# The experts' first layer turned around: its hidden units on partitions, each tile's weights first copied to a fixed place

## The chip, the cores and the metric

The kernel runs on one core of a Trainium2 chip. The metric is the device time of one execution in microseconds (us). The core has five engines that run their own instruction streams and meet at semaphores: TensorE (PE in the profile, its weight loads PEld), VectorE (DVE), ScalarE (ACT), GpSimd (POOL) and SyncE (SP, which here issues most of the transfers).

## The reference

Two decoder layers on 4 sequences of 512 tokens of width 128, in float32. Each layer has self-attention, cross-attention to 77 context vectors, and a feed-forward part, each behind a layer norm and added to the residual. The feed-forward part of the first layer is a mixture of 8 experts, of which each token uses its two best:

```python
weights, indices = jax.lax.top_k(gate_logits, 2)
weights = jax.nn.softmax(weights, axis=-1)
h = einsum('bsd,edh->ebsh', x, w1) + b1      # 128 -> 1024 per expert
xh, gh = split(h, 2)                         # plain half, gated half: 512 each
act = silu(gh) * xh
out_e = einsum('ebsf,efd->ebsd', act, w2) + b2   # 512 -> 128
# the outputs of a token's two experts, weighed and summed
```

## The kernel before

The kernel is one program without loops at run time. Its first stream is the first layer's self-attention (A0) and cross-attention (X0), cut into 32 units of four heads. Then comes the expert stage (M0), then a second stream with self-attention (A1), cross-attention and feed-forward of the second layer.

**First stream.** For each unit SP loads the stacked queries and keys into one of four slots of the tile `stk` (`load_sp`, lines 638 and 644), and TensorE can't begin the unit's row maxima (L574) until both have landed. Between these loads SP issues, two per unit and in the order of a list called `later`, the weights that later stages need (`unit_sp`, L1173), and one piece of the experts' weights per unit (L2257). All these transfers go through one SP queue. One entry of `later` is the bias `b_gated`, the gated half of the experts' first bias, broadcast to all 128 partitions: 2 MB.

**Expert stage.** The 4096 pairs of token and expert are sorted by expert on the chip. GpSimd writes each token's normalised row to a region of its expert in device memory (`scatter_pool`, L1726: 32 indirect DMAs). Then 39 tiles of 128 rows follow, each of one expert. Which expert is known only at run time, so the engines read ten codes into registers (`codes`, L1686), each code holding the experts of four tiles, and address weights and biases through registers. A tile t goes through these steps:

1. SP loads its rows into `x_in` (L1833), TensorE transposes them (`turn`, L1753), and DVE copies the result to SBUF and computes where the outputs go (`turned`, L1637 and L1638).
2. TensorE multiplies them with the expert's first weights (`hidden`, L1759), the gated half (z=1) and the plain half (z=0). The rows stand on the partitions of the result, the 512 units on its free axis. Each half is one matmul of 128x512 in the program, which the profile shows as two instructions (float32).
3. DVE adds the gated bias (`gated`, L1644), ACT applies Silu (`gate_part`, L1802).
4. DVE adds the plain bias (L1651) and multiplies by the gate (L1655), both in `product`.
5. TensorE transposes the four 128x128 blocks of the activations (`turn_act`, L1767), ACT copies them to SBUF (`turned_act`, L1806), and TensorE multiplies them with the second weights (`output`, L1774: four accumulating matmuls, eight instructions).
6. DVE adds the second bias (L1661), and GpSimd scatters the tile's rows to device memory (L1742, an indirect DMA).

The order on each engine is written out by hand. TensorE: gated half of t+1, transposes of t's activations, `turn` of t+2, plain half of t+1, output of t. DVE: gated bias of t+1, `turned` of t+2, product of t+1, output bias of t. GpSimd does nothing in the stage but the scatter of each tile. An engine issues its instructions strictly in this order, so a wait holds everything behind it.

Of the kernel before, what the change touches and what calls it, by code (L numbers as in the profile page):

```python
# [11 lines left out]
F32 = mybir.dt.float32  # L12
# [239 lines left out]
def build(nc, d, out):  # L252
# [4 lines left out]
    with es:  # L257
# [71 lines left out]
        b1_gated = sb("b1_gated", [P, NE, FF])  # L329
        b1_plain = stk[:].rearrange("p u z h n -> p (u z h n)").bitcast(F32).rearrange("p (e n) -> p e n", e=NE)  # L330
# [1152 lines left out]
        def second_stream_sp(e):  # L1483
# [13 lines left out]
            diff expo plus recip gates zeroed scattered xT xT_out gated_half gated plain_half plain silu act actT actT_out y_in y_out  # L1497
# [86 lines left out]
        def moe_dve(e, ln):  # L1584
# [50 lines left out]
            def turned(t):  # L1635
                e.wait_ge(m["xT"], t + 1)
                e.tensor_copy(x_inT[:, t % 2], bank_misc[:, 0:P]).then_inc(m["xT_out"], 1)  # L1637
# [3 lines left out]
            def gated(t, ex):  # L1641
                k = t % 2
                e.wait_ge(m["gated_half"], t + 1)
                e.tensor_tensor(silu[:, k], hid[k][1], b1_gated[:, bass.ds(ex[t], 1)].rearrange("p o n -> p (o n)"), ALU.add)\  # L1644
                    .then_inc(m["gated"], 1)
# [18 lines left out]
            e.wait_ge(s_biases, 16 * 2)  # L1664
# [5 lines left out]
            gated(0, ex)  # L1670
            product(0, ex)
            for t in range(BUSY_TILES):
                if t + 1 < BUSY_TILES:
                    if t + 1 not in ex:
                        ex |= experts(code, t + 1)
                    gated(t + 1, ex)
# [29 lines left out]
        act = oT[:, 0]  # L1706
        actT = okT
# [5 lines left out]
        hid = [(bank_max[0], bank_max[1]), (bank_st[1], bank_st[2])]  # L1713
        y_bank = bank_st[0]
        t_bank = bank_st[3]
# [21 lines left out]
        def moe_pool(e, ln):  # L1737

            for t in range(BUSY_TILES):
                e.wait_ge(m["y_at"], t + 1)  # L1740
                e.wait_ge(m["y_out"], FREE + t + 1)
                e.indirect_dma_start(scr_y, bass.IndirectOffsetOnAxis(ap=y_at[:, t:t + 1], axis=0),  # L1742
                                     y_sb[:, t % 2], None).then_inc(m["stored"][t % 2], 16)

        def moe_pe(e, ln):
            weights_pe(e)
            e.wait_ge(m["tile_e"], CODED + 2)
            code = codes(e)

            def turn(t):  # L1750
                e.wait_ge(m["tile_in"][t % 2], 16 * (t // 2 + 1))
                wait(e, m["xT_out"], t)
                e.transpose(bank_misc[:, 0:P], x_in[:, t % 2, 0:D], ident[:]).then_inc(m["xT"], 1)  # L1753

            def hidden(t, ex, z):
# [3 lines left out]
                e.matmul(hid[t % 2][z], x_inT[:, t % 2],  # L1759
                         w1[:, bass.ds(ex[t], 1), z * FF:(z + 1) * FF].rearrange("p o n -> p (o n)"),  # L1760
                         start=True, stop=True).then_inc(m["gated_half" if z else "plain_half"], 1)

            def turn_act(t):
                e.wait_ge(m["act"], t + 1)
                wait(e, m["actT_out"], t)
                for c in range(FC):
                    mm = e.transpose(t_bank[:, c * P:(c + 1) * P], act[:, c * P:(c + 1) * P], ident[:])  # L1767
                mm.then_inc(m["actT"], 1)

            def output(t, ex):  # L1770
                e.wait_ge(m["actT_out"], t + 1)
                e.wait_ge(m["y_out"], FREE + t)
                for c in range(FC):
                    mm = e.matmul(y_bank[:, 0:D], actT[:, c * P:(c + 1) * P],  # L1774
                                  w2[:, bass.ds(ex[t], 1), c, :].rearrange("p o n -> p (o n)"), start=(c == 0), stop=(c == FC - 1))
# [5 lines left out]
            ex = experts(code, 0)  # L1781
            for z in (1, 0):
                hidden(0, ex, z)
            for t in range(BUSY_TILES):
                if t + 1 < BUSY_TILES:
                    if t + 1 not in ex:
                        ex |= experts(code, t + 1)
                    hidden(t + 1, ex, 1)
                turn_act(t)
                if t + 2 < BUSY_TILES:  # L1790
                    turn(t + 2)
                if t + 1 < BUSY_TILES:
                    hidden(t + 1, ex, 0)
                output(t, ex)

        def moe_act(e, ln):
            e.wait_ge(m["diff"], 1)
            e.activation(gate_t[:, 1], gate_t[:, 0], ACT.Exp).then_inc(m["expo"], 1)

            def gate_part(t):  # L1800
                e.wait_ge(m["gated"], t + 1)
                e.activation(silu[:, t % 2], silu[:, t % 2], ACT.Silu).then_inc(m["silu"], 1)  # L1802

            def turned_act(t):
                e.wait_ge(m["actT"], t + 1)
                e.copy(actT[:], t_bank).then_inc(m["actT_out"], 1)  # L1806

            gate_part(0)
            for t in range(BUSY_TILES):
                turned_act(t)  # L1810
                if t + 1 < BUSY_TILES:
                    gate_part(t + 1)
# [150 lines left out]
        def weights_pe(e):  # L1963
            e.wait_ge(f["abs"], 2)
# [274 lines left out]
        halves = d["M0_b1"].rearrange("o (e z n) -> o e z n", e=NE, z=2)  # L2239
        later += [(b1_gated[:], halves[:, :, 1].to_broadcast([P, NE, FF]))]  # L2240
# [148 lines left out]
```

## Time and profile before

| | |
|---|---|
| median of 3 runs | 846.29 us (845.27 to 852.08) |
| profiled execution, span from first to last instruction | 844.2 us |
| first half-matmul of the expert stage to end of its last scatter | 371.8 to 504.7 us |

| busy, us (share of the span) | |
|---|---|
| PE | 689.9 (82%) |
| DVE | 589.3 (70%) |
| ACT | 414.1 (49%) |
| POOL | 285.0 (34%) |

The profile shows one execution and gives no other time for it than its span, so what lies around the span is taken as the 2.1 us between it and the median. The shares are means over stages that have different limits; what the change does is read in the stretches where it acts. The TensorE clock that the chip granted has two levels, 1.2 GHz (0.50) and 2.4 GHz (1.00); over the whole span its mean is 0.88.

### The profile page before, as it was taken

How to read it: one execution, taken by the hardware profiler on the slowest of the kernel's cores; microseconds unless marked ns; L12 is line 12 of the kernel's file. 1: busy time of each engine (PE TensorE's matmuls, PEld its weight loads, DVE VectorE, ACT ScalarE, POOL GpSimd, SP SyncE). 2: the span in 40 equal slices, each digit the busy share in tenths (PEclk: the TensorE clock that was granted, in tenths of full speed). 3: DMA queues.
4: the chain of work that ended last, by engine and by line, in shares of the span. 5: the costliest groups of instructions: out<-in, count | busy, mean ns of one | idle time of the engine just before them, and what ended most of it. 6: DMA issues, size and time to landing. Idle time of an engine off the chain costs nothing.

```text
span 844.2 us, 14947 instructions
## 1 busy us (share of the span) xinstructions
PE 689.9 (82%) x4693; PEld 333.1 (39%) x4698; DVE 589.3 (70%) x1606; ACT 414.1 (49%) x708; POOL 285.0 (34%) x504
## 2 busy tenths in 40 slices
PE   2759999989888998239999973668899988999887
PEld 1334454444434445116666641212232322324443
DVE  3757678686646664738788753778889898962664
ACT  1332556555665443003333322137688787885454
POOL 4742454543532233723222320122423133230310
PEclk9875999998988657569999995559999999999998
DMA  7443665482232314311111113521122210000000
GB/s 217 150 176 107 190 183 155 125 262 78 83 93 53 94 47 128 96 36 38 43 41 45 39 29 105 169 75 52 63 90 89 64 52 26 26 2 1 0 26 26
DMA packets 74780, 71.27 MB, mean 84 GB/s; under 512 B 14560, under 2 KB 67168, under 8 KB 74704
## 3 DMA queue, kind: packets, MB, share of 16 engines
q1 hardware_dynamic: 72000, 64.84, 25.1%
q0 software_dynamic: 2272, 4.69, 1.8%
q8 instruction: 40, 0.66, 0.3%
q10 hardware_dynamic: 432, 0.79, 0.3%
q14 instruction: 36, 0.29, 0.1%
HBM read 41.90 MB, written 28.00 MB: 83 GB/s over the span
## 4 chain that ended last, share of the span: by engine, by line
PE 62%; DVE 18%; issue 7%; POOL 4%; DMA 4%; ACT 4%; SPq 1%; DVEq 0%; POOLq 0%; ACTq 0%
PE bank_pv L732 11%; DVE mx L590 9%; PE bank_turn L574 8%; PE bank_scores L2024 5%; PE bank_scores L684 4%; PE bank_scores L1774 4%; PE bank_turn L1759 4%; PE bank_scores L1759 4%; PE bank_turn L751 3%; POOL routed_tokens L1726 2%; PE bank_scores L1767 2%; PE bank_turn L793 2%; PE bank_turn L528 2%; DMA stk<-stack_A 1%; DVE stats L450 1%
## 5 line engine op out<-in xcount | busy, mean ns | idle before, releaser
L590 DVE TENSOR_REDUCE mx<-bank_turn 128x1 f32<-128x512 f32 (+3 forms) x452 | 260.6, 616 | 67.2 <-PE bank_turn L579 35.8
L574 PE MATMUL bank_turn<-stk 64*128 64x77 bf16 (+4 forms) x708 | 164.2, 314 | 29.4 <-DVE mx L590 17.7
L684 PE MATMUL bank_scores<-stk 64*128 64x512 bf16 (+4 forms) x576 | 176.4, 372 | 4.8 <-ACT probs L705 3.6
L709 ACT ACTIVATE probs<-bank_scores 128x1024 f32<-128x1024 f32 (+4 forms) x160 | 117.2, 768 | 111.7 <-PE bank_scores L684 111.4
L705 ACT ACTIVATE probs<-bank_scores 128x512 f32<-128x512 f32 x256 | 138.6, 605 | 35.3 <-PE bank_scores L684 34.3
L732 PE MATMUL bank_pv<-probs,vsl 128*32 128x512 f32 (+4 forms) x1152 | 143.0, 570 | 2.8 <-POOL probs L717 1.9
L574 PEld LDWEIGHTS bank_turn<-stk 64*128 64x128 bf16 x708 | 54.4, 102 | 134.5 <-DVE mx L590 63.2
L717 POOL TENSOR_SCALAR_AFFINE_SELECT probs<-probs 128x256 f32<-128x256 f32 x128 | 52.1, 410 | 78.1 <-ACT probs L709 76.8
L1742 POOL DMA_INDIRECT expert_outputs<-probs,y_at x39 | 37.4, 960 | 101.0 <-DVE probs L1661 98.0
L477 POOL TENSOR_TENSOR rstd<-var,mhalf 128x4 f32<-128x4 f32 x24 | 25.4, 1058 | 119.2 <-DVE var L456 119.1
L1806 ACT COPY okT<-bank_scores 128x512 f32<-128x512 f32 x39 | 22.9, 587 | 80.8 <-PE bank_scores L1767 80.8
L528 PE MATMUL bank_turn<-ident,xn 128*128 128x128 f32 x60 | 13.2, 358 | 57.0 <-DVE xn L471 57.0
L684 PEld LDWEIGHTS bank_scores<-stk 64*128 64x128 bf16 (+1 forms) x576 | 47.6, 97 | 30.0 <-ACT probs L705 18.0
L579 PE MATMUL bank_turn<-behind_even,even_q 64*128 64x128 bf16 x256 | 53.4, 230 | 0.0
L578 PE MATMUL bank_turn<-behind_pair,pair_q 64*128 64x128 bf16 x256 | 53.4, 230 | 0.0
L1774 PEld LDWEIGHTS bank_scores<-w,okT 128*128 128x128 f32 x312 | 37.7, 191 | 25.0 <-issue 25.0
L2024 PE MATMUL bank_scores<-f_w1c,w 128*128 128x512 f32 x96 | 46.0, 616 | 0.4 <-ACT w L537 0.4
L1774 PE MATMUL bank_scores<-w,okT 128*128 x312 | 43.9, 284 | 0.8 <-ACT okT L1806 0.8
L604 POOL CAST neg<-mx 128x16 bf16<-128x16 f32 x33 | 6.5, 198 | 111.5 <-DVE mx L590 98.1
L590 DVE TENSOR_REDUCE mx<-bank_scores 128x1 f32<-128x512 f32 x60 | 40.8, 680 | 3.0 <-PE bank_scores L574 2.9
L1759 PE MATMUL bank_turn<-w,probs 128*128 x80 | 42.5, 616 | 0.0
L542 ACT COPY xnT<-bank_turn 128x512 f32<-128x512 f32 x19 | 11.1, 584 | 56.9 <-PE bank_turn L528 56.9
(299 smaller groups left out, 1179.7 us busy)
## 6 DMA issues: line engine op xcount, KB each, us to landing
stk<-stack_A SPq DMA_DIRECT2D x64, 256.0 KB, 3.2
w<-in_M_w SPq DMA_DIRECT2D x12, 512.0 KB, 4.7
stack_A<-parts SPq DMA_DIRECT2D x15, 384.0 KB, 3.1
stack_A<-fill SPq DMA_DIRECT2D x8, 512.0 KB, 5.1
stk<-stack_X SPq DMA_DIRECT2D x16, 256.0 KB, 2.7
stack_A<-parts SPq DMA_DIRECT2D x15, 256.0 KB, 3.2
probs<-routed_tokens SPq DMA_DIRECT2D x39, 65.0 KB, 1.8
b_gated<-in_M_b SPq DMA_DIRECT2D x1, 2048.0 KB, 11.9
```

The costliest lines, as they stand in the source:

```text
L574: mm = e.matmul(o, stk[r, slot, 0, pp, qt * P:(qt + 1) * P], stk[r, slot, 1, pp, 0:keys], start=True, stop=not a.causal)
L578: e.matmul(o, half(pair_q, j), half(behind_pair, j), start=False, stop=False)
L579: mm = e.matmul(o, half(even_q, j), half(behind_even, j), start=False, stop=True)
L590: e.tensor_reduce(o.rearrange("p h q -> p q h"), bank_of((g, m))[:, 0:k * keys].rearrange("p (q h k) -> p q h k", q=len(tiles), h=len(hs)) ...
L684: mm = e.matmul(score_bank(g, kt, i)[0:a.kp, 0:S - q0], stk[r, slot, 1, pp, kt * P:kt * P + a.kp], stk[r, slot, 0, pp, q0:S], start=True, ...
L705: e.activation(probs[:, probs_of(g, kt), j + 2 * pp], score_bank(g, kt, i), ACT.Exp, scale=1 / math.sqrt(HD)).then_inc(s["probs"], 1)
L709: e.activation(probs[0:a.kp, probs_of(g, kt), j:HG:2, 0:n], bank_scores[0:a.kp, 2 * j:2 * j + 2, 0:n], ACT.Exp, scale=1 / math.sqrt(HD)).t ...
L717: e.affine_select(out=o, in_=o, compare_op=ALU.is_ge, fill=0.0, base=0, pattern=[[0, 2], [1, P]], channel_multiplier=-1).then_inc(s["maske ...
L732: mm = e.matmul(bank_pv[VW * h:VW * (h + 1), q0:S], vsl[0:a.kp, slot, kt, h, :], probs[0:a.kp, probs_of(g, kt), h, 0:S - q0], start=(kt == ...
L1759: e.matmul(hid[t % 2][z], x_inT[:, t % 2], w1[:, bass.ds(ex[t], 1), z * FF:(z + 1) * FF].rearrange("p o n -> p (o n)"), start=True, stop=T ...
L1774: mm = e.matmul(y_bank[:, 0:D], actT[:, c * P:(c + 1) * P], w2[:, bass.ds(ex[t], 1), c, :].rearrange("p o n -> p (o n)"), start=(c == 0), ...
L2024: e.matmul(bank, f_xT[:, b, j * P + tap:j * P + tap + P], f_w1c[:, tap], start=(tap == 0), stop=False)
```

## The change

Layout: the first layer's weights become the stationary operand and the tokens the moving one, so the 512 units of a half come out on partitions, in four blocks of 128, and the tokens on the free axis. This is the layout that the second layer needs: `turn_act` and `turned_act` (L1767, L1806) go. A bias is now one value per partition: ACT adds the gated bias inside Silu, DVE adds the plain bias inside the product, each in four instructions, one per block of 128 units. The bias is loaded as 64 rows of 128 and transposed once by TensorE; the two broadcast loads of 2 MB (`b_gated` in `later`, and `b1_plain` at the start of `moe_sp`, L1816) go.

Weights: GpSimd copies the 128x1024 first weights of a tile's expert into one of two fixed places (`w_now`), so TensorE's first layer needs no registers. GpSimd now reads the codes itself. Its order is: copy of t+2, scatter of t, copy of t+3, scatter of t+1, and so on; ACT reads the codes too.

Order: DVE keeps `turned` of t+2, product of t+1, output of t. TensorE keeps gated half of t+1, `turn` of t+2, plain half of t+1, output of t. `act` is double, the gated half has one bank, the plain half two.

```diff
+        w_now = sb("w_now", [P, 2, 2 * FF])
+        b1_rows = sb("b1_rows", [NE * 2 * FC, P])
+        b1_cols = sb("b1_cols", [P, NE, 2 * FC])
...
             def product(t, ex):
                 e.wait_ge(m["plain_half"], t + 1)
-                wait(e, m["act"], t)
-                e.tensor_tensor(act[:], hid[k][0], b1_plain[:, bass.ds(ex[t], 1)].rearrange("p o n -> p (o n)"), ALU.add)\
-                    .then_inc(m["plain"], 1)
-                e.wait_ge(m["plain"], t + 1)
                 e.wait_ge(m["silu"], t + 1)
-                e.tensor_tensor(act[:], act[:], silu[:, k], ALU.mult).then_inc(m["act"], 1)
+                wait(e, m["y_in"], t - 1)
+                for c in range(FC):
+                    cols = slice(c * P, (c + 1) * P)
+                    i = e.scalar_tensor_tensor(act[:, k, cols], plain_bank[k][:, cols],
+                                               b1_cols[:, bass.ds(ex[t], 1), c], silu[:, k, cols], ALU.add, ALU.mult)
+                i.then_inc(m["act"], 1)
...
-            gated(0, ex)
             product(0, ex)
...
         def moe_pool(e, ln):
+            def weights(t, ex):
+                wait(e, m["plain_half"], t - 1)
+                e.tensor_copy(w_now[:, t % 2], w1[:, bass.ds(ex[t], 1)].rearrange("p o n -> p (o n)")).then_inc(m["w_now"], 1)
+
+            e.wait_ge(s_experts, 16 * W_PIECES)
+            e.wait_ge(m["tile_e"], CODED + 2)
+            code = codes(e)
+            ex = experts(code, 0)
+            for t in range(2):
+                weights(t, ex)
             for t in range(BUSY_TILES):
+                if t + 2 < BUSY_TILES:
+                    if t + 2 not in ex:
+                        ex |= experts(code, t + 2)
+                    weights(t + 2, ex)
                 e.wait_ge(m["y_at"], t + 1)
                 e.wait_ge(m["y_out"], FREE + t + 1)
                 e.indirect_dma_start(scr_y, bass.IndirectOffsetOnAxis(ap=y_at[:, t:t + 1], axis=0),
                                     y_sb[:, t % 2], None).then_inc(m["stored"][t % 2], 16)
...
+            def hidden(t, z):
+                k = t % 2
                 if z == 1:
+                    e.wait_ge(m["w_now"], t + 1)
                     e.wait_ge(m["xT_out"], t + 1)
+                    wait(e, m["silu"], t)
+                else:
                     wait(e, m["act"], t - 1)
+                bank = gated_bank if z else plain_bank[k]
+                for c in range(FC):
+                    at = z * FF + c * P
+                    mm = e.matmul(bank[:, c * P:(c + 1) * P],
+                                  w_now[:, k, at:at + P], x_inT[:, k], start=True, stop=True)
+                mm.then_inc(m["gated_half" if z else "plain_half"], 1)
...
         def moe_act(e, ln):
+            e.wait_ge(m["b1_in"], 1)
+            e.copy(b1_cols[:].rearrange("p e c -> p (e c)"), bank_max[0][:, 0:NE * 2 * FC]).then_inc(m["b1_out"], 1)
...
+            def gate_part(t, ex):
+                k = t % 2
+                e.wait_ge(m["gated_half"], t + 1)
+                wait(e, m["act"], t - 1)
+                for c in range(FC):
+                    cols = slice(c * P, (c + 1) * P)
+                    i = e.activation(silu[:, k, cols], gated_bank[:, cols], ACT.Silu,
+                                     bias=b1_cols[:, bass.ds(ex[t], 1), FC + c])
+                i.then_inc(m["silu"], 1)
...
         def moe_sp(e):
-            e.dma_start(b1_plain, halves[:, :, 0].to_broadcast([P, NE, FF])).then_inc(s_biases, 16)
...
         def weights_pe(e):
+            e.transpose(bank_max[0][:, 0:NE * 2 * FC], b1_rows[:], ident[0:NE * 2 * FC, 0:NE * 2 * FC]).then_inc(m["b1_in"], 1)
...
-        later += [(b1_gated[:], halves[:, :, 1].to_broadcast([P, NE, FF]))]
+        later += [(b1_rows[:], d["M0_b1"].rearrange("o (r p) -> (o r) p", p=P))]
```

## Rows read from the trace of the kernel before

**Rows 1.** Busy time by stretch: us, PE, PEld, DVE, ACT, POOL (instructions), clock, DMA share, GB/s.

```profile
381.00:490.00 109.00, 108.86 (x572) 67.15 (x571) 87.47 (x203) 39.37 (x68) 32.64 (x34) 1.00 0.16 42
260.00:270.00 10.00, 7.62 (x80) 3.82 (x76) 8.28 (x36) 5.99 (x9) 2.58 (x4) 1.00 0.39 93
```

**Rows 2.** Timeline of one tile's period: start, length, engine, line, idle before it.

```profile
423.89 1.12 PE L1774 MATMUL bank_scores<-w,okT 128*128 x8
424.85 1.02 PE L1759 MATMUL bank_turn<-w,probs 128*128 x2
424.91 0.69 DVE L1655 TENSOR_TENSOR oT<-oT,probs 128x512 f32<-128x512 f32 x1
425.52 0.28 DVE L1661 TENSOR_TENSOR probs<-bank_scores,rest 128x128 f32<-128x128 f32 x1
425.71 0.60 PE L1767 MATMUL bank_scores<-ident,oT 128*128 128x128 f32 x4
426.10 0.69 DVE L1644 TENSOR_TENSOR probs<-bank_turn,b_gated 128x512 f32<-128x512 f32 x1 [0.29 <-PE bank_turn L1759]
426.15 0.27 PE L1753 MATMUL bank_turn<-ident,probs 128*128 128x128 f32 x1
426.26 1.02 PE L1759 MATMUL bank_turn<-w,probs 128*128 x2
426.35 0.59 ACT L1806 COPY okT<-bank_scores 128x512 f32<-128x512 f32 x1 [2.05 <-PE bank_scores L1767]
426.56 0.96 POOL L1742 DMA_INDIRECT expert_outputs<-probs,y_at  x1 [2.27 <-DVE probs L1661]
427.12 1.12 PE L1774 MATMUL bank_scores<-w,okT 128*128 x8
```

**Rows 3.** Timelines of ACT and of DVE elsewhere: runs of 128x128 instructions.

```profile
673.38 1.14 ACT L1951 ACTIVATE w<-bank_scores,x_rec 128x128 f32<-128x128 f32 x4 [1.11 <-PE bank_scores L1942]
...
511.00 2.19 DVE L1700 SCALAR_TENSOR_TENSOR x_sb<-w,gate,x_sb 128x128 f32<-128x128 f32 x8 [8.00 <-DMA w<-expert_outputs]
```

**Rows 4.** Groups of POOL instructions: count, then busy us, mean ns of one, idle before.

```profile
L1255 POOL TENSOR_TENSOR probs<-probs 128x512 f32<-128x512 f32 x8 | 10.1, 1270 | 8.5 <-DVE probs L1241 8.5
L657 POOL COPY vsl<-routed_rows 128x128 f32<-128x128 f32 x32 | 9.3, 291 | 0.0
L884 POOL CAST parts<-cos_sin 128x512 bf16<-128x512 f32 x8 | 4.9, 614 | 10.8 <-ACT cos_sin L865 10.8
```

**Rows 5.** Timeline of POOL and of PE at the start of the expert stage.

```profile
365.33 0.96 POOL L1726 DMA_INDIRECT routed_tokens<-routed_rows,place_u  x1 [0.30 <-issue]
...
371.78 3.47 PE L1759 MATMUL bank_turn<-w,probs 128*128 x4
...
381.00 0.96 POOL L1742 DMA_INDIRECT expert_outputs<-probs,y_at  x1 [14.70 <-DVE probs L1661]
```

**Rows 6.** Line 1686, TensorE's sequencer reading codes: ns min/median/max, first and last start.

```profile
L1686 PEldq TENSOR_LOAD <-tile_e x10: 295/307/498, 356.5 to 362.7; - x10
```

**Rows 7.** Timeline of SP and of PE around 174 to 189 us.

```profile
173.82 0.57 SPq L1173 DMA_DIRECT2D b_gated<-in_M_b  x1
...
188.52 0.23 PE L574 MATMUL bank_turn<-stk 64*128 64x128 bf16 x1 [2.74 <-DMA stk<-stack_A]
```

**Rows 8.** The chain that ended last: its longest piece between 170 and 200 us.

```profile
176.17 12.31 DMA stk<-stack_A
```

**Rows 9.** Busy time of the stretch behind that piece; columns as in the first group.

```profile
190.00:203.00 13.00, 12.75 (x96) 6.00 (x97) 6.74 (x14) 6.45 (x11) 3.53 (x10) 0.74 0.26 87
```

**Rows 10.** Timeline of PE: the one L611 instruction of units 7, 9, 11 and 13.

```profile
138.14 0.22 PE L611 MATMUL bank_turn<-identb,neg 128*32 128x128 bf16 x1 [0.24 <-DVE mx L590]
...
158.78 0.23 PE L611 MATMUL bank_turn<-identb,neg 128*32 128x128 bf16 x1
...
179.60 0.22 PE L611 MATMUL bank_turn<-identb,neg 128*32 128x128 bf16 x1 [0.24 <-DVE mx L590]
...
205.03 0.23 PE L611 MATMUL bank_turn<-identb,neg 128*32 128x128 bf16 x1
```

More of the change, by code:

```diff
@@ L1496, in build @@
             place placed zero_at zeros tokens floor cum tile_le tile_held tile_f tile_at tile_row tile_e y_at
-            diff expo plus recip gates zeroed scattered xT xT_out gated_half gated plain_half plain silu act actT actT_out y_in y_out
+            diff expo plus recip gates zeroed scattered xT xT_out w_now b1_in b1_out gated_half plain_half silu act y_in y_out
             weighed""".split()}
@@ L1662, in output @@
                     .then_inc(m["y_out"], 1)
-            e.wait_ge(s_biases, 16 * 2)
+            e.wait_ge(s_biases, 16)
+            e.wait_ge(m["b1_out"], 1)
             e.wait_ge(m["tile_e"], CODED + 2)
@@ L1752, in turn, with output @@
                 wait(e, m["xT_out"], t)
-                e.transpose(bank_misc[:, 0:P], x_in[:, t % 2, 0:D], ident[:]).then_inc(m["xT"], 1)
-            def hidden(t, ex, z):
+                e.transpose(x_bank[:, 0:P], x_in[:, t % 2, 0:D], ident[:]).then_inc(m["xT"], 1)
+            def hidden(t, z):
+                k = t % 2
                 if z == 1:
+                    e.wait_ge(m["w_now"], t + 1)
                     e.wait_ge(m["xT_out"], t + 1)
+                    wait(e, m["silu"], t)
+                else:
                     wait(e, m["act"], t - 1)
[L1759 to L1763, printed above, removed]
-                e.wait_ge(m["act"], t + 1)
[L1765 to L1771, printed above, removed]
+                bank = gated_bank if z else plain_bank[k]
[4 more added lines that the diff above has]
+                mm.then_inc(m["gated_half" if z else "plain_half"], 1)
+            def output(t, ex):
+                e.wait_ge(m["act"], t + 1)
                 e.wait_ge(m["y_out"], FREE + t)
                 for c in range(FC):
-                    mm = e.matmul(y_bank[:, 0:D], actT[:, c * P:(c + 1) * P],
+                    mm = e.matmul(y_bank[:, 0:D], act[:, t % 2, c * P:(c + 1) * P],
                                   w2[:, bass.ds(ex[t], 1), c, :].rearrange("p o n -> p (o n)"), start=(c == 0), stop=(c == FC - 1))
@@ L1780, in moe_pe @@
                 turn(t)
-            ex = experts(code, 0)
+            ex = {}
             for z in (1, 0):
-                hidden(0, ex, z)
+                hidden(0, z)
             for t in range(BUSY_TILES):
                 if t + 1 < BUSY_TILES:
[L1786 to L1789, printed above, removed]
+                    hidden(t + 1, 1)
                 if t + 2 < BUSY_TILES:
@@ L1792, in moe_pe @@
                 if t + 1 < BUSY_TILES:
-                    hidden(t + 1, ex, 0)
+                    hidden(t + 1, 0)
+                if t not in ex:
+                    ex |= experts(code, t)
                 output(t, ex)
         def moe_act(e, ln):
+            e.wait_ge(m["b1_in"], 1)
+            e.copy(b1_cols[:].rearrange("p e c -> p (e c)"), bank_max[0][:, 0:NE * 2 * FC]).then_inc(m["b1_out"], 1)
             e.wait_ge(m["diff"], 1)
             e.activation(gate_t[:, 1], gate_t[:, 0], ACT.Exp).then_inc(m["expo"], 1)
[L1800 to L1808, printed above, removed]
+            def gate_part(t, ex):
[7 more added lines that the diff above has]
+                i.then_inc(m["silu"], 1)
+            e.wait_ge(m["b1_out"], 1)
+            e.wait_ge(m["tile_e"], CODED + 2)
+            code = codes(e)
+            ex = {}
             for t in range(BUSY_TILES):
-                turned_act(t)
-                if t + 1 < BUSY_TILES:
-                    gate_part(t + 1)
+                if t not in ex:
+                    ex |= experts(code, t)
+                gate_part(t, ex)
         def moe_sp(e):
             e.wait_ge(s["scores"], exps_at(2 * UN))
-            e.dma_start(b1_plain, halves[:, :, 0].to_broadcast([P, NE, FF])).then_inc(s_biases, 16)
             e.dma_start(b2, d["M0_b2"].rearrange("o (e d) -> o e d", e=NE).to_broadcast([P, NE, D])).then_inc(s_biases, 16)
```

18 lines of the change are left out of this document (3 added, 15 removed).

## The prediction

> **What bounds the kernel now.** I began with the busy shares and the chain that ended last. TensorE leads in both, but these are means over stages with different limits, so I went on to the stretches that the change touches: the expert stage, and the one place in the first stream where a removed transfer was in flight.
>
> In the expert stage TensorE is busy in 108.86 of 109 us at the full clock [rows 1]. The timeline of one period says the same in detail [rows 2]: the output's eight instructions start at 423.89, the gated half at 424.85, the transposes of the activations at 425.71, the turn of the next rows at 426.15, the plain half at 426.26, the next output at 427.12. That is 0.96 + 0.86 + 0.44 + 0.11 + 0.86 = 3.23 us a tile, each group starting when the one before has streamed through. DVE's product ends (424.91 + 0.69 = 425.60) 0.11 us before the transposes start, so DVE is near the bound too. GpSimd is idle 2.27 us in each period, and its scatter starts 0.76 us after DVE's output (425.52 + 0.28 = 425.80, to 426.56). Nothing waits for it. The stage as a whole is 371.78 to 381.96 for the first tile's way to the end of its scatter [rows 5], 10.2 us, and 38 x 3.23 = 122.7 us for the rest.
>
> **TensorE's side of the change.** Each half becomes eight 128-column instructions with eight weight loads, the shape of the output's, which take 0.96 [rows 2]. The 0.44 of transposes go. New period if TensorE set it: 3 x 0.96 + 0.11 = 2.99 us, 0.24 less than now. Its matmul columns stay the same; only transposes are lost.
>
> **What takes its place: a loop through GpSimd.** I followed the order of each queue. `w_now` has two places. GpSimd copies the weights of t+3 only behind the scatter of t, which waits for DVE's output of t. On DVE that output stands behind the product of t+1, which needs Silu of t+1, which needs the gated half of t+1. And the gated half of t+3 needs the copy. So from the gated half of t+1 to that of t+3, two periods, this chain must run:
>
> - eight matmul instructions, start to end: 1.12 [rows 2].
> - to ACT: 0.04 behind a matmul with fixed operands (426.31 to 426.35), 0.23 where DVE reads two registers first (425.87 to 426.10) [rows 2]. I take 0.15, as the bias is addressed by a register.
> - four Silu of 128x128 with a bias column: 1.14, from four activations of this shape with a scale column [rows 3]. One Silu of 512 columns is to be replaced by this.
> - to DVE: 0.15 again.
> - four products of 128x128: eight like them took 2.19 [rows 3], so about 1.1 and the last one's tail: 1.14.
> - the output bias, which begins before the product's end: 425.60 to 425.80, 0.20 [rows 2].
> - to the scatter 0.76, the scatter 0.96 [rows 2].
> - the copy of 1024 columns. No row has it. A one-input copy of 128 columns took 0.291 and one of 512 took 0.614 [rows 4], so 0.32 more for 384 columns; 1024 give 0.614 + 512 x 0.00084 = 1.05. An addition with two inputs takes 1.27 for 512 [rows 4], 2.54 for 1024, the upper bound. I take 1.05, since this has one input. The wait and the register work of the copy I cost at nothing, as the 0.96 of the scatter covers them; without that cover they cost about 0.3, what stands between two scatters [rows 5].
> - back to TensorE: 0.11 (425.60 to 425.71) [rows 2].
>
> Sum: 1.12 + 0.15 + 1.14 + 0.15 + 1.14 + 0.20 + 0.76 + 0.96 + 1.05 + 0.11 = 6.78 us for two tiles, 3.39 a tile. This is above 2.99, so TensorE waits about 0.4 us a tile for `w_now`, and the period grows by 0.16: 38 x 0.16 = **+6.1 us**. With both handoffs at 0.04 it is 6.56 (3.28), with both at 0.23 and the 0.3 uncovered 7.24 (3.62).
>
> The Trainium skill, GPSIMD Engine Reference, section 3.1 (Elementwise), gives a best case of about 1.8 cycles per element for a tight loop at 1.2 GHz, and 1.03 for bodies of up to two operations. By the first, 1024 columns take 1.54 us (an estimate from that page), the loop 7.27, and the sum below would be 858; the rows are with the second.
>
> **The start of the stage.** GpSimd must now read the ten codes, and it can begin only when its last scatter of tokens is issued (365.33) or over (366.29) [rows 5]. TensorE's ten reads took 6.2 us for nine [rows 6], so 6.9. Then a copy, 1.05, and 0.11: the first gated half can start at 373.4 to 374.4 instead of 371.78. I take **+2.0 us**. ACT reads its codes in the same time and is idle there. The first tile's own way is two halves at the low clock, 3.47 [rows 5], and then the loop's links up to its scatter's end, 5.62, with about 0.5 for a next gated half that is still slow: 9.6 instead of 10.2, **-0.6 us**.
>
> **The removed loads.** `b_gated` (2 MB) is issued at 173.82, ahead of the next unit's queries and keys on the same queue; those landed 12.31 us after their issue [rows 7, 8]. TensorE sat idle 2.74 us for them [rows 7], and in the stretch behind it the clock was 0.74, so 6.8 of 13 us at half speed [rows 9], worth up to 3.4 us. The gain lies between 0 (other loads fill the queue as well) and 6.1. The period of the units repeats every four units, so I compare units 12 and 13 with 8 and 9: from 179.60 to 205.03 it is 25.43, from 138.14 to 158.78 it is 20.64 [rows 10]. I take the difference, **-4.8 us**. The other broadcast (`b1_plain`) lies beside GpSimd's row of token scatters, which ends at 366.29 [rows 5] and sets the start whatever else lands: nothing. So does the single transpose and copy of the bias; without that cover they cost well under 1 us.
>
> **Sum.** 844.2 + 6.1 + 2.0 - 0.6 - 4.8 = 846.9 us of span. The median stands 2.1 above the span, which I add: 849.0.
>
> **Rivals.**
>
> *TensorE keeps the pace (faster).* If the loop is shorter than 2 x 2.99 = 5.98, the period falls to 2.99: 38 x -0.24 = -9.1, with the other terms -12.5, so 833.8. That wants 0.8 us less, as if GpSimd prepared the scatter while it waits. For it: two scatters in a row stand 0.30 apart, not 0.76 [rows 5]; that alone makes the loop 6.32 and the time 840. Against: in this stage every scatter follows a wait, and 0.76 is what follows that wait [rows 2]. Chance 0.16.
>
> *The copy is dear (slower).* Place: GpSimd, between scatter and gated half. From a copy of 1.36 us on (loop 7.09, +5.8 over my sum) the kernel is over 1% slower; at 1.54 it takes 858, at the two-input bound of 2.54 the loop is 8.27 and the time 877. The register work behind the scatter, if not covered, counts the same way. For it: no row has a copy of this size or with a register in its address. Against: the slope of two one-input rows [rows 4]. Chance 0.22.
>
> *The loads' stall stays*, because the next entry and the 512 KB of weights take `b_gated`'s place: 849.0 + 4.8 = 853.8. For it: the queue held both at that time. Against: 2 MB of it are gone. Chance 0.14.
>
> *The clock falls in the stage*: each instruction of TensorE at half speed makes its period about 5.9, and the stage some 100 us longer. Against: a stretch with TensorE busy 7.62 of 10 us had the full clock [rows 1], and here it would be 2.99 of 3.39. Chance 0.04.
>
> **How the numbers follow.** My forecast has 0.44, with its own range from 843 to 854 by the loop's bounds. The range of 8 in 10 is 836 to 862: it reaches into the faster rival and past a copy of 1.54, and leaves out the far ends (about 0.06 below, 0.12 above). About 1%, 8.5 us, is what a measurement can tell from no change. Faster: the first rival but for its slow part, and a little of the forecast, 0.16. Slower: the second rival, the clock, and the edge of the third, 0.31. Within 1%: 0.53.
>
> **What would show it.** Right: a period of about 3.4 us; TensorE idle before the gated half, released by GpSimd's copy; the copy near 1.05 and close behind the scatter; the first gated half near 374; the wait of 2.74 for `stk` gone. Wrong: a period of 3.0 with TensorE back to back, a copy of 1.4 or more, a gap between scatter and copy, the wait for `stk` still there, or a clock below 1.00 in the stage.

## The result, and the profile after

| | before | after |
|---|---|---|
| median, same chip, 4 runs each | 845.78 us (840.49 to 852.08) | 855.46 us (851.13 to 856.31) |
| profiled execution: time, span | 846.29, 844.2 | 855.75, 853.9 |
| first gated half to the end of the last scatter | 371.8 to 504.7 | 368.4 to 513.6 |
| period of the expert stage (first to last scatter's start, over 38) | 3.230 | 3.504 |

The ratio is 1.0107, with a 95% interval from 1.0065 to 1.0148: slower, by about the 1% that the text called measurable. The time lies in the range of 836 to 862 and outside the forecast's own range of 843 to 854.

First the stage as a whole, and two stretches of the first stream, in the windows of the changed kernel (columns as in [rows 1]):

```profile
190.00:203.00 13.00, 12.44 (x130) 6.50 (x126) 8.37 (x18) 7.36 (x12) 5.92 (x15) 1.00 0.31 103
215.00:320.00 105.00, 94.92 (x713) 46.36 (x714) 61.78 (x257) 54.57 (x74) 34.93 (x67) 0.72 0.23 66
...
382.00:490.00 108.00, 90.41 (x761) 86.69 (x760) 68.04 (x211) 34.43 (x120) 61.66 (x61) 1.00 0.14 38
```

In the stage TensorE is no longer busy throughout: 90.41 of 108 us, where it was 108.86 of 109 [rows 1]. The clock stays at 1.00. GpSimd has gone from 32.64 of 109 to 61.66 of 108, and no engine is full. That is the picture of a loop of handoffs, and the groups of instructions say what TensorE waits for (columns as in [rows 4]):

```profile
L1772 PE MATMUL bank_scores<-probs,w_now 128*128 128x128 f32 x624 | 86.4, 287 | 21.6 <-POOL w_now L1733 20.5 <-ACT probs L1813 1.1
L1733 POOL COPY w_now<-w 128x1024 f32 x39 | 40.8, 1047 | 7.4 <-PE bank_scores L1772 7.3
L1748 POOL DMA_INDIRECT expert_outputs<-probs,y_at x39 | 38.1, 978 | 64.4 <-PE bank_scores L1772 25.7 <-DVE y_at L1639 18.7 <-DVE probs L1657 17.6
L1639 DVE SCALAR_TENSOR_TENSOR y_at<-probs,tile_f 128x1 uint32<-128x1 f32 x39 | 27.8, 712 | 0.0
```

Of 21.6 us that TensorE's first layer stood idle, 20.5 ended with GpSimd's copy. The copy takes 1047 ns. The last line is a surprise, taken up at the end: a DVE instruction on 128x1 elements takes 712 ns on the mean.

The loop itself, for one pair of tiles, in the timeline of the changed kernel (start, length, engine, line, idle before it):

```profile
431.59 1.16 PE L1772 MATMUL bank_scores<-probs,w_now 128*128 128x128 f32 x8 [1.23 <-POOL w_now L1733]
...
433.02 1.14 ACT L1813 ACTIVATE probs<-bank_scores,b_cols 128x128 f32<-128x128 f32 x4 [3.24 <-PE bank_scores L1772]
433.10 1.30 DVE L1639 SCALAR_TENSOR_TENSOR y_at<-probs,tile_f 128x1 uint32<-128x1 f32 x1
433.33 1.05 POOL L1733 COPY w_now<-w 128x1024 f32 x1
434.48 1.11 PE L1772 MATMUL bank_scores<-probs,w_now 128*128 128x128 f32 x8
434.51 1.13 DVE L1649 SCALAR_TENSOR_TENSOR oT<-bank_scores,b_cols,probs 128x128 f32<-128x128 f32 x4
...
435.56 0.28 DVE L1657 TENSOR_TENSOR probs<-bank_scores,rest 128x128 f32<-128x128 f32 x1
...
436.59 0.98 POOL L1748 DMA_INDIRECT expert_outputs<-probs,y_at  x1 [2.22 <-PE bank_scores L1772]
...
437.57 1.05 POOL L1733 COPY w_now<-w 128x1024 f32 x1
...
438.68 1.16 PE L1772 MATMUL bank_scores<-probs,w_now 128*128 128x128 f32 x8 [1.19 <-POOL w_now L1733]
```

Read it from gated half to gated half: matmuls 1.16, 0.27 to ACT, Silu 1.14, 0.35 to DVE, product 1.13, output's end 0.20 later, 0.75 to the scatter, scatter 0.98, copy 1.05 with nothing between, 0.06 to TensorE. That is 7.09 us for two tiles; the gated half between them (434.48) uses the other place of `w_now`, filled at 434.38, and follows TensorE's output without idle time. Over all 38 periods the mean is 3.504, a little under 7.09 / 2, as the last two have no copy to wait for (2.79 and 2.05).

The start of the stage, in the timeline of the changed kernel, and behind it the groups of its line 1681, in which each engine's sequencer reads the codes (ns min/median/max, first and last start):

```profile
361.97 0.96 POOL L1718 DMA_INDIRECT routed_tokens<-routed_rows,place_u  x1 [0.30 <-issue]
362.93 2.02 POOL L1733 COPY w_now<-w 128x1024 f32 x2
367.03 0.45 PE L1759 MATMUL bank_pv<-ident,probs 128*128 128x128 f32 x1 [13.55 <-DMA probs<-routed_tokens]
368.36 3.62 PE L1772 MATMUL bank_scores<-probs,w_now 128*128 128x128 f32 x16
370.47 1.28 ACT L1813 ACT_TABLE_LOAD   x1 [20.35 <-PE bank_scores L1772]
371.77 1.14 ACT L1813 ACTIVATE probs<-bank_scores,b_cols 128x128 f32<-128x128 f32 x4
...
379.43 0.98 POOL L1748 DMA_INDIRECT expert_outputs<-probs,y_at  x1 [6.12 <-DVE y_at L1639]
```

```profile
L1681 POOLq TENSOR_LOAD <-tile_e x10: 283/294/513, 352.7 to 358.3; - x10
L1681 PEldq TENSOR_LOAD <-tile_e x10: 294/304/494, 353.7 to 359.9; - x10
```

GpSimd's sequencer read the ten codes from 352.7 to 358.3, while its scatters of tokens went on to 362.93 on the engine. Right behind the last of them stand the first two copies. So the codes cost nothing. Nor do the copies, which end at 364.95: TensorE's first `turn` waits until 367.03 for its rows to land. The first gated half comes 5.43 us after the last token scatter's end, as before (366.29 to 371.78, 5.49 [rows 5]). In the first tile's way there is a new item: the table load for Silu, 1.28 us, right behind the first gated half.

The units of the first stream, in the timeline of the changed kernel (units 11 and 13; line 612 is the L611 of [rows 10]):

```profile
178.41 0.22 PE L612 MATMUL bank_turn<-identb,neg 128*32 128x128 bf16 x1 [0.24 <-DVE mx L591]
...
185.22 0.21 PE L575 MATMUL bank_turn<-stk 64*128 64x128 bf16 x1 [0.64 <-DVE mx L591]
...
199.05 0.23 PE L612 MATMUL bank_turn<-identb,neg 128*32 128x128 bf16 x1
```

Units 12 and 13 take 20.64 us instead of 25.43 [rows 10], the wait of 2.74 for `stk` is gone (0.64 is left, ended by DVE), and the clock behind it is 1.00 instead of 0.74 [rows 9].

**The balance of the two spans.** End of the last token scatter 3.36 us earlier; from there to the first gated half 0.06 less; from there to the end of the first scatter 12.05 instead of 10.18, 1.87 more; pace 38 x 0.274 = 10.41 more; behind the stage 0.85 more. Sum +9.7, and 853.9 - 844.2 = 9.7.

### The profile page after: what moved, and what is told of

The parts are those of the page before. It is cut to its first block, busy times and chain, and to the rows that moved or that the text cites. A ratio compares the mean times of both kernels' runs of the same rounds, so it can differ in the third digit from the quotient of the medians.

```text
span 853.9 us, 16085 instructions
## 1 busy us (share of the span) xinstructions
PE 684.5 (80%) x5006; PEld 371.3 (43%) x5011; DVE 573.5 (67%) x1645; ACT 413.1 (48%) x787; POOL 325.1 (38%) x543
## 4 chain that ended last, share of the span: by engine, by line
PE 51%; DVE 20%; issue 10%; POOL 8%; ACT 5%; DMA 3%; POOLq 1%; SPq 1%; DVEq 1%; ACTq 0%
PE bank_pv L733 11%; DVE mx L591 10%; PE bank_turn L575 7%; PE bank_scores L2036 5%; PE bank_scores L1772 4%; PE bank_scores L685 4%; PE bank_turn L752 3%; POOL w_now L1733 2%; POOL expert_outputs L1748 2%; PE bank_turn L794 2%; POOL routed_tokens L1718 2%; PE bank_turn L529 2%; ACT probs L1813 2%; DVE stats L451 2%; DVE xn L472 1%
## 5 line engine op out<-in xcount | busy, mean ns | idle before, releaser
L1772 PE MATMUL bank_scores<-probs,w_now 128*128 128x128 f32 x624 | 86.4, 287 | 21.6 <-POOL w_now L1733 20.5
L1772 PEld LDWEIGHTS bank_scores<-probs,w_now 128*128 128x128 f32 x624 | 78.9, 199 | 26.1 <-POOL w_now L1733 24.5
L1813 ACT ACTIVATE probs<-bank_scores,b_cols 128x128 f32<-128x128 f32 x156 | 44.7, 368 | 91.7 <-PE bank_scores L1772 91.6
L1649 DVE SCALAR_TENSOR_TENSOR oT<-bank_scores,b_cols,probs 128x128 f32<-128x128 f32 x156 | 44.1, 343 | 30.4 <-PE bank_scores L1772 23.0
L1733 POOL COPY w_now<-w 128x1024 f32 x39 | 40.8, 1047 | 7.4 <-PE bank_scores L1772 7.3
L1780 PE MATMUL bank_scores<-w,oT 128*128 x312 | 42.0, 278 | 1.5 <-DVE probs L1657 1.5
```

Of the source, the lines that this page charges most:

```text
L1733: e.tensor_copy(w_now[:, t % 2], w1[:, bass.ds(ex[t], 1)].rearrange("p o n -> p (o n)")).then_inc(m["w_now"], 1)
L1772: mm = e.matmul(bank[:, c * P:(c + 1) * P], w_now[:, k, at:at + P], x_inT[:, k], start=True, stop=True)
L1813: i = e.activation(silu[:, k, cols], gated_bank[:, cols], ACT.Silu, bias=b1_cols[:, bass.ds(ex[t], 1), FC + c])
```

## The experiments

Medians of "before" are of runs on the same chip beside each group of kernels: 845.42 for e1, e2, e3 and e5, 845.50 for e4 and e6 to e8, 846.38 for e9 to e11, 847.84 for e12. The period is from the first to the last scatter's start, over 38; "way" is from the first gated half to the first scatter's start.

| | median us | ratio to before, 95% | period | way |
|---|---|---|---|---|
| after | 855.46 | 1.0107 [1.0065, 1.0148] | 3.504 | 11.07 |
| e1, output first | 840.84 | 0.9942 [0.9903, 0.9981] | 3.199 | 8.93 |
| e2, three places | 829.04 | 0.9820 [0.9781, 0.9859] | 2.809 | 9.72 |
| e3, before, its load moved | 846.58 | 1.0013 [0.9984, 1.0043] | 3.232 | 9.58 |
| e4, table early | 856.18 | 1.0128 [1.0092, 1.0164] | 3.503 | 9.35 |
| e5, fixed bias | 846.24 | 1.0018 [0.9980, 1.0057] | 3.315 | 8.52 |
| e6, load back | 852.48 | 1.0105 [1.0062, 1.0148] | 3.500 | 9.73 |
| e7, three places, table | 829.24 | 0.9807 [0.9762, 0.9852] | 2.813 | 9.29 |
| e8, e7 with output first | 842.30 | 0.9968 [0.9937, 0.9999] | 3.163 | 7.91 |
| e9, e8 with one input | 838.65 | 0.9882 [0.9821, 0.9942] | 3.178 | 8.48 |
| e10, e1 with one input | 842.29 | 0.9950 [0.9907, 0.9992] | 3.199 | 8.93 |
| e11, after with one input | 853.74 | 1.0086 [1.0047, 1.0124] | 3.499 | 11.08 |
| e12, half copies | 847.42 | 0.9992 [0.9944, 1.0039] | 3.297 | 10.86 |

**Is it the loop through GpSimd's copy?** e1, e2 and e12 each open the loop at another place, e5 shortens two of its handoffs.

e1, in DVE's order:
```diff
+                output(t, ex)
                 if t + 1 < BUSY_TILES:
                     product(t + 1, ex)
-                output(t, ex)
```


> The changed kernel with one order turned on DVE: the output bias of tile t before the product of tile t+1. Theory (a loop of two tiles through GpSimd's queue: gated half, Silu, product, output bias, scatter, copy, gated half, 7.1 us): Silu and product leave the loop; what is left runs over TensorE's gated half, turn, plain half and output (2.95), then 0.2 + 0.28 + 0.76 + 0.98 + 1.05 + 0.06 = 6.3 us for two tiles, a period of 3.15 instead of 3.50, so 13 us less than the changed kernel: about 842. Rival (GpSimd's own work, or the many small instructions on ACT and DVE, set the pace): the period stays at 3.5 and the time at 855.

e2, in `w_now` and GpSimd's order (the index becomes `t % 3`, the wait for `plain_half` t - 2):
```diff
-        w_now = sb("w_now", [P, 2, 2 * FF])
+        w_now = sb("w_now", [P, 3, 2 * FF])
...
-            for t in range(2):
+            for t in range(3):
                 weights(t, ex)
...
-                    weights(t + 2, ex)
+                    weights(t + 3, ex)
```


> The changed kernel with three places for the copied weights instead of two, so that GpSimd copies three tiles ahead. Theory (loop through the queue): the same 7.1 us now serve three tiles, 2.4 a tile, and TensorE sets the pace with 2.99 to 3.05: 17 to 19 us less than the changed kernel, 836 to 838. Rival (GpSimd's work or its sharing of SBUF with DVE sets the pace): the period stays above 3.3, 848 or more.

e12, in GpSimd's copy (`hidden` waits for 2t+1 and 2t+2):
```diff
-                e.tensor_copy(w_now[:, t % 2], w1[:, bass.ds(ex[t], 1)]...).then_inc(m["w_now"], 1)
+                for z in (1, 0):
+                    cols = slice(z * FF, (z + 1) * FF)
+                    e.tensor_copy(w_now[:, t % 2, cols], w1[:, bass.ds(ex[t], 1), cols]...).then_inc(m["w_now"], 1)
```


> The changed kernel with GpSimd's copy cut in two, the gated half's 512 columns first, each half of TensorE's first layer waiting for its own. Theory of the loop: only the first half-copy lies between the scatter and the gated half. By a row of 0.614 for a copy of 512 columns that is 0.43 less in 7.13 us for two tiles: period 3.50 to 3.28, 8.2 us in total, to about 847. Rival: the loop has slack elsewhere, or the plain half now waits for the second copy (it ends about 0.6 us later, while the gated half takes 0.89): the period stays at 3.5 or falls by under 0.1.

e5, in `product` (and likewise in `gate_part`):
```diff
-                                               b1_cols[:, bass.ds(ex[t], 1), c], silu[:, k, cols], ALU.add, ALU.mult)
+                                               b1_cols[:, 0:1, c], silu[:, k, cols], ALU.add, ALU.mult)
```


> The changed kernel with the first layer's biases of expert 0 for every tile, so that Silu and product read a fixed column and no register (this leaves out the choice of the bias). Theory (the period is above my 3.39 because the register instructions behind the waits make the two handoffs 0.28 and 0.35 instead of 0.15): handoffs of 0.05 to 0.1, loop 6.6, period 3.3, 7 to 8 us less than the changed kernel: 847 to 848. Rival (the handoffs are long for another reason, such as DVE's address instruction that is stretched beside the copy): the period falls by less than 0.05, 853 to 855.

All four periods fell about as the loop asks; that e1's 3.199 lies near its 3.15 has another reason, told further down. e2's window of the stage has TensorE full:

```profile
382.00:480.00 98.00, 97.99 (x868) 97.48 (x867) 57.99 (x243) 39.95 (x140) 70.04 (x70) 1.00 0.19 48
```

Its period of 2.809 is below the 2.99 that was computed for TensorE: eight instructions follow each other in 0.89 here, 0.1115 each, and 3 x 0.89 + 0.11 = 2.78. The 0.96 was taken from the output's row, where the second of the eight starts 0.18 behind the first (423.89 to 424.07) and the others follow at 0.11. In e12 the half copies take 622 ns (the groups of its instructions):

```profile
L1735 POOL COPY w_now<-w 128x512 f32 x78 | 45.7, 622 | 7.1 <-PE bank_scores L1776 7.1
```

That takes 1.05 - 0.62 = 0.43 out of the loop, 0.21 of a period, and the period fell by 0.207. In e5 the two handoffs shrink, as its timeline shows (matmuls' end 430.33 to ACT 0.04, Silu's end 431.51 to DVE 0.09):

```profile
429.27 1.06 PE L1772 MATMUL bank_scores<-probs,w_now 128*128 128x128 f32 x8
...
430.37 1.14 ACT L1813 ACTIVATE probs<-bank_scores,b_cols 128x128 f32<-128x128 f32 x4 [1.65 <-PE bank_scores L1772]
...
431.60 1.13 DVE L1649 SCALAR_TENSOR_TENSOR oT<-bank_scores,b_cols,probs 128x128 f32<-128x128 f32 x4 [0.71 <-PE bank_scores L1772]
```

That is 0.23 and 0.26 less than 0.27 and 0.35, 0.25 a tile by the loop; the period fell by 0.19, as on every fourth tile of e5 the handoff to DVE is still 0.32 to 0.47: the loop takes 6.60 and about 6.83 by turns. So a bias addressed by a register costs 0.4 to 0.5 us per pair of tiles in this loop. The time goes into register instructions of the two sequencers, which stand between the end of the wait and the first instruction of the engine. Here they are for the two handoffs of the pair above (432.76 to 433.03 for ACT, 434.20 to 434.52 for DVE), and last for the handoff of 0.23 in the kernel before (425.88 to 426.09); columns are ns min/median/max, first and last start:

```profile
L1813 ACTq ALU_OP  x2: 38/38/38, 432.8 to 432.8; - x2
L1813 ACTq FUSED_REGOPS  x1: 60/60/60, 432.9 to 432.9; - x1
L1649 DVEq ALU_OP  x2: 45/45/45, 434.3 to 434.3; - x2
L1649 DVEq FUSED_REGOPS  x1: 57/57/57, 434.4 to 434.4; - x1
...
L1644 DVEq ALU_OP  x1: 45/45/45, 425.9 to 425.9; - x1
L1644 DVEq FUSED_REGOPS  x1: 57/57/57, 426.0 to 426.0; - x1
```

Three stand there now, two before. e5's rival, that DVE's stretched address instruction makes the handoff long, falls with e11 below: there the instruction takes 0.27 on every tile, and the handoff to DVE is 0.35 as before.

**What bounds the other order?** With three places the copy is off the path, and then e1's order should make no difference: e8 tries both together.

e7 is e2 with the first line below; e8 is e7 with e1's order.
```diff
+            e.activation(silu_first[:], ones_row[0:1, 0:1], ACT.Silu)
             e.wait_ge(m["b1_out"], 1)
```


> Three places for w_now and the early Silu table together. By the theory of the loop the copy is off the path (period 2.81, TensorE back to back) and only the table load is left in the first tile's way: 829.0 - 1.3 = 827.7. Rival: with three places the second and third copy also stand on GpSimd ahead of the first scatter, and the table load is hidden by that: no change from 829.

> The former with DVE's output of t ahead of the product of t+1. If TensorE bounds the stage at 2.81 already, the order gives nothing: 827 to 828, period 2.81. Rival: DVE's order still decides when TensorE can begin the output, and the period moves by 0.1 or more either way (4 us in total); the product starting later would then make the output of t+1 late.

e7 equals e2 (829.24 and 829.04): the way fell by 0.43 only, and four runs each can't tell the 1.3 us that were expected from nothing. e8 did not stay at 2.81: its period is 3.163, and 842.30 is 13 us worse than e7. Its groups show the address instruction held as in the changed kernel, but on nearly every tile:

```profile
L1640 DVE SCALAR_TENSOR_TENSOR y_at<-probs,tile_f 128x1 uint32<-128x1 f32 x39 | 52.1, 1335 | 0.0
```

So I took this for the new bound, and tested it by writing the instruction with one tensor input:

```diff
-                e.scalar_tensor_tensor(y_at[:, t:t + 1], x_in[:, t % 2, D + 1:D + 2], tile_f[:, t:t + 1], x_in[:, t % 2, D:D + 1],
-                                       ALU.not_equal, ALU.add).then_inc(m["y_at"], 1)
+                e.tensor_scalar(y_at[:, t:t + 1], x_in[:, t % 2, D + 1:D + 2], tile_f[:, t:t + 1], x_in[:, t % 2, D:D + 1],
+                                ALU.not_equal, ALU.add).then_inc(m["y_at"], 1)
```


> e8 (three places, early table, DVE's output of t ahead of the product of t+1) with DVE's address instruction written as one with a single tensor input and two scalar columns. Theory: in e8 GpSimd's copy holds this instruction (1.2 to 1.55 us instead of 0.21), and the output of the next tile stands behind it, so the period is output, scatter, copy, output = 3.16. Without the hold DVE's way output, product, TensorE's output, output is left: period 2.85 to 3.0, the total 6 to 12 us below e8. Rival: the hold is only a sign of something else that paces DVE (or a scalar column is held as well): the period stays at 3.16 and the total at 842.

> e1 (two places, DVE's output of t ahead of the product of t+1) with the same single-input address instruction. Theory: e1's period of 3.20 is the same held instruction (output 430.62, scatter 431.67, copy 432.65, held to 433.72, output 433.78 in its trace); without it 2.9 to 3.05, the total 6 to 11 us below e1's 840.8. Rival: in e1 the copy into one of two places is the limit by itself, and the period stays at 3.2.

> The changed kernel with the same single-input address instruction and nothing else. There the product behind the held instruction starts 0.1 us later anyway, as it waits for ACT, so the period stays at 3.50 and the total at 855. Rival: the hold delays the product in the loop, and the period falls by up to 0.1 (4 us in total).

The hold went, in e9's groups

```profile
L1640 DVE TENSOR_SCALAR y_at<-probs,tile_f 128x1 uint32<-128x1 f32 x39 | 10.4, 266 | 0.0
```

and the periods stayed: 3.178, 3.199 and 3.499. (e9's median is 3.7 us below e8's, with spreads of 6 and 10 us and ratios whose intervals just meet, while its profiled span is 4.4 us longer; the total leaves it open.) My theory that the hold paces e1 and e8 fell. What does can be read from e10's timeline, though no run tries it by itself:

```profile
430.42 1.14 PE L1780 MATMUL bank_scores<-w,oT 128*128 x8
...
431.70 0.29 DVE L1657 TENSOR_TENSOR probs<-bank_scores,rest 128x128 f32<-128x128 f32 x1 [1.30 <-PE bank_scores L1780]
432.09 1.13 DVE L1649 SCALAR_TENSOR_TENSOR oT<-bank_scores,b_cols,probs 128x128 f32<-128x128 f32 x4
...
433.62 1.13 PE L1780 MATMUL bank_scores<-w,oT 128*128 x8
```

With the output ahead of the next product, DVE waits 1.30 for TensorE's output, and TensorE's next output waits for the product behind it: 0.14 + 0.39 + 1.13 + 0.40 + 1.14 = 3.20 us per tile. In e1 and e8 the held instruction ended just when TensorE's output did, two chains of nearly one length; my 2.85 to 3.0 had left out the register work at both handoffs. The changed kernel's own order avoids this chain, and with three places it is the better one.

**The first tile's way.** e4 has the extra line of e7 on the changed kernel.

> One Silu of a single element stands behind ACT's last Exp ahead of the stage, so the table for Silu loads there. If the load of 1.28 us behind the first gated half is on the path to the first scatter, the way from the first gated half to the first scatter's start falls from 11.07 to about 9.8 us and the total by 1.3 (to about 854). Rival: the first tile waits for something else (the plain half at the low clock, the second copy), the way stays near 11 and the total unchanged. The period stays at 3.50 in both.

The table load moved from 370.47 to 350.46, as the timeline of ACT in e4 shows, and the way fell by 1.72, from 11.07 to 9.35:

```profile
350.46 1.28 ACT L1818 ACT_TABLE_LOAD   x1
...
370.80 1.14 ACT L1814 ACTIVATE probs<-bank_scores,b_cols 128x128 f32<-128x128 f32 x4 [18.84 <-PE bank_scores L1773]
```

So the load was on the path. Part of the 1.72 is the clock: it rose to 1.00 at 377.0 in the changed kernel, 8.7 us behind the first gated half, at 374.0 in e4 (5.3) and at 370.0 in e6 (3.4), whose way is 9.73 with the table load still in it. So of the 1.72 no more than 1.28 is the load itself, and the two are not told apart further. The median did not fall (856.18): 1.7 us is less than the spread of these runs, and in e4's profile the time behind the stage is 1.7 us longer than in the changed kernel's, so the total leaves it open.

**The loads.** e3 is the kernel before with its 2 MB `b_gated` moved out of `later` to the start of the stage, beside `b1_plain`; e6 is the changed kernel with a load of 1.25 MB put into that slot.
```diff
+            e.dma_start(b1_gated[:], halves[:, :, 1].to_broadcast([P, NE, FF])).then_inc(s_biases, 16)
...
-        later += [(b1_gated[:], halves[:, :, 1].to_broadcast([P, NE, FF]))]
+        later += [(b1_rows[:], d["M0_b1"].rearrange("o (r p) -> (o r) p", p=P))]
```


> The kernel before with one thing changed: the 2 MB broadcast of the gated bias leaves its place among the loads of the first stream and is issued behind that of the second bias, at the start of the expert stage; a load of 32 KB that nothing reads takes its place. Theory (the stall of the queries and keys is due to these 2 MB): the wait of 2.74 us is gone, units 12 and 13 take 20.6 instead of 25.4 us; later the TensorE clock gives some of it back, so 841 to 844. Rival (the other loads fill the queue): units 12 and 13 stay at 24 or more, 846.

```diff
+        spare = sb("spare", [P, 5, FF])
...
-        later += [(b1_rows[:], d["M0_b1"].rearrange("o (r p) -> (o r) p", p=P))]
+        later += [(spare[:], halves[:, 0:5, 1].to_broadcast([P, 5, FF]))]
```


> The changed kernel with a broadcast load of 1.25 MB (five eighths of the removed one, read by nothing) put back in the slot of b_gated; the rows of the bias come at the stage's start instead. Theory that the removal gains, but the low clock gives it back later: units 12 and 13 take 23 to 25.4 us instead of 20.64, units 15 to 31 fall from 96.7 to about 94, and the total stays within 2 us of the changed kernel's 855. Rival, the removal is worth its 4.8 us (3.0 for five eighths): the total rises to 858 or 860.

From the timelines (L611 or its like) and the windows from 215 to 320 of each profile:

| | units 12, 13 | units 12 to 31 | clock in 215:320 |
|---|---|---|---|
| before | 25.43 | 138.8 | 0.77 |
| after | 20.64 | 136.8 | 0.72 |
| e3 | 20.64 | 140.5 | 0.69 |
| e2 | 20.64 | 139.5 | 0.69 |
| e1 | 20.64 | 133.2 | 0.76 |
| e6 | 20.63 | 132.9 | 0.77 |

e3 shows that the load alone makes the stall: without it units 12 and 13 take 20.64. But its total does not fall, 1.0013 with an interval from 0.9984 to 1.0043. (Its profiled execution, 852.48, is the longest of its ten runs.) What comes later moves: the same units take from 132.9 to 140.5 us in kernels whose program is the same there, longer the lower the clock. In e6 my expectation missed. TensorE waits 0.64 there, in its timeline,

```profile
186.78 0.21 PE L576 MATMUL bank_turn<-stk 64*128 64x128 bf16 x1 [0.64 <-DMA stk<-stack_A]
```

which is no more than the 0.64 that it waits for DVE in the changed kernel, without this load. Units 12 and 13 take 20.63, and the clock behind them stays at 1.00 (its windows):

```profile
190.00:203.00 13.00, 12.45 (x128) 6.05 (x125) 8.76 (x18) 8.82 (x14) 5.27 (x14) 1.00 0.32 104
```

so 1.25 MB cost nothing in these units. The 2 MB cost 2.74 - 0.64 = 2.1 of waiting and a clock of 0.74 behind it [rows 7, 9]. How e6 differs in total from the changed kernel stays open: the intervals are the same, and the phases of the clock differ by more than the load.

## Why the prediction was right or wrong

**The bound and the loop: right.** TensorE waits for GpSimd's copy, the copy stands right behind the scatter, and three places, half the copy, or a fixed bias move the period by what the loop says (e2, e12, e5).

**The pace, +6.1: mis-sized, 10.4.** The loop measured 7.09 against 6.78. Matmuls +0.04; to ACT 0.27 instead of 0.15, +0.12; to DVE 0.35 instead of 0.15, +0.20; scatter and the way to it +0.01; product -0.01; copy right; to TensorE 0.06 instead of 0.11, -0.05. That is the whole 0.31 in the pair shown; in the mean over the stage 3.504 - 3.39 = 0.11 a tile is left of it, which makes the 4.3 us between 6.1 and 10.4. The term that was mis-sized is "I take 0.15, as the bias is addressed by a register": the row with registers gave 0.23 [rows 2], and even that was too little, as three register instructions stand behind the wait here and two in that row. The upper end of the bounds, 3.62, held it.

**The copy, 1.05: right**, 1.047 measured, and its register work is covered by the scatter. The Trainium skill, GPSIMD Engine Reference, section 3.1 (Elementwise), offered two rates; this copy goes by its 1.03 cycles for short bodies: from 622 ns for 512 columns to 1047 for 1024 is 0.83 ns a column, 1.0 cycle at that page's 1.2 GHz. The estimate of 1.54 was the wrong one of the two.

**The start, +2.0: wrong, -0.1.** The failed step is that GpSimd "can begin only when its last scatter of tokens is issued". Its sequencer read the codes while scatters still stood ahead on the engine (352.7 to 358.3, scatters to 362.93), and the copies were done before the first tile's rows had landed.

**The first tile, -0.6: wrong, +1.9.** Left out was ACT's table load, 1.28 us on the path. Before it came early (352.9), and so it does in e5, whose Silu has no register (356.8; way 8.52). With the register the wait for TensorE comes first and the load behind it. The clock rose late as well (377.0; before 374.8), which the 0.5 for "a next gated half that is still slow" did not cover.

**The loads, -4.8: right in their place, -3.4 at the stage's start.** Units 12 and 13 gave exactly 20.64. But over units 12 to 31 only 2.0 of the 4.8 are left, since the later units ran at a lower clock, 0.72 instead of 0.77 in 215:320, which the sum had taken as fixed; another 1.2 us was there already at unit 11 (178.41 instead of 179.60), and that is no effect of the change: in the experiments unit 11 comes anywhere from 178.07 to 181.04. What is left of the gain differs as much from one profiled execution to the next, from 5.6 us (e1, 133.2) to a loss of 1.7 (e3, 140.5) against the 138.8 of before; the median of e3 shows none.

**Not in the sum:** +0.9 behind the stage. The errors together: 4.3 - 2.1 + 2.5 + 1.4 + 0.9 = 7.0, from 846.9 to the measured span of 853.9. All errors but one are too low and come to 9.1; that the start took 2.1 of them back was chance.

**The rivals.** TensorE sets the pace only with a third place, in e2 and e7, and there the kernel is faster than before. The copy is not dear, the stall of the loads did not stay, and the clock did not fall in the stage. The mechanism of the forecast was the true one, and its own range was too narrow at the upper end, since it took the handoffs at a middle value. The sum had the kernel 2.7 us slower and it came out 9.7 slower, so the outcome fell just outside "within 1%" (0.53) and into "slower" (0.31).

**A version that beats both** is the one in which TensorE does set the pace, as in the first rival: the changed kernel with three places, 829.04, 0.9820 of before (0.9781 to 0.9859).

## What to carry to other kernels

When a wait is made between two engines, close the loop through every queue, write it out link by link, and ask how many buffers it spans: here a third buffer of 512 KB turned +1% into -2%. Price a handoff by whether the consumer has register work behind its wait: it cost 0.04 and 0.09 without and 0.27 and 0.35 with. A stall removed ahead of a stretch of changing clock need not show in the total: the 4.8 us gained here in two units were no longer to be seen in e3's median.

## What the runs showed of the hardware

- **A DVE instruction held by GpSimd.** The address instruction with two tensor inputs in SBUF, 128x1, took 0.21 in the kernel before and 1.0 to 1.76 on 18 of 39 tiles in the changed kernel, each time ending 0.02 to 0.03 us after a GpSimd copy's end (433.10 + 1.30 = 434.40, copy's end 434.38). With one tensor input and scalar columns it took 0.26 to 0.27 on all tiles, beside scatters and copies alike (e9 to e11). The Trainium skill, SBUF — State Buffer, section "Who interferes with whom", says that a DVE instruction with two SBUF inputs contends with a GpSimd instruction that reads SBUF, and one with at most one SBUF input, outside DVE's 2-port modes, does not; the traces agree. On 17 of these 18 tiles the instruction began while the scatter ahead of the copy still ran, and in the kernel before 35 of 39 began beside a scatter and were not held; why a copy that has not begun holds it was not tried. Nor does the hold always last to a copy's end: in e12, with half copies, it took 0.34 to 0.62 on nine tiles and ended 0.01 to 0.02 us before the first half copy began. Taking the hold away shortened no period by more than 0.005 us (e9 to e11).
- **The sequencer of GpSimd runs ahead.** It had read the last code at 358.6, while its engine still had indirect DMAs to go until 362.93.
- **Small matmuls back to back.** 128-column float32 matmuls with a weight load each follow one another every 0.1115 us in e2's stage, at a clock of 1.00; only the first of some outputs takes longer (0.17 for the one at 431.70). Over the window from 382 to 480 that is 868 in 97.99 us, 0.113 each.
